# A Mamba-2 and FFN block on one core: Y turned by DVE and DMA in place of TensorE, the output projection in halves, part of the decay split on POOL

## The reference, cut to what matters

```python
xn = layernorm(x)                                  # x: (2, 2048, 512)
xb, z = split(xn @ in_proj_w.T)                    # 1024 each
xb = silu(causal_conv4(xb) + conv_b)
X, dt, B, C = split(xb @ x_proj_w.T)               # 16 heads of 64; B, C of 128
dt = softplus(dt @ dt_proj_w.T + dt_proj_b);  A = -exp(A_log) * dt
Y = scan of the state (decay exp(cumsum A), B, C, X * dt) + X * D
attn = (Y * silu(z)) @ out_proj_w.T                # 1024 -> 512
q(w) = clip(round(w / mean|w|), -1, 1)
ffn = (sigmoid(xn @ q(w1).T) * (xn @ q(w2).T)) @ q(w3).T    # 1408 hidden
out = x + attn + ffn
```

## Time and profile before

| | us |
|---|---|
| median of 3 runs | 1666.37 (1664.38 to 1667.06) |
| the profiled execution, its own time | 1663.81 |
| its span, first to last instruction | 1662.0 |
| busy in it: PE, DVE, ACT, POOL | 1600.7, 1126.5, 895.1, 540.0 |
| mean granted clock of TensorE | 0.987 of full |

### The profile page before, as it was taken

How to read it: one execution, slowest core, us unless ns; L and a number is a source line. 1 busy time by engine, 2 the same in 40 slices (tenths; PEclk the granted TensorE clock), 3 DMA queues, 4 the chain that set the end, 5 groups by cost and what they waited for, 6 DMA issues and landing times.

```text
span 1662.0 us, 25592 instructions
## 1 busy us (share of the span) xinstructions
PE 1600.7 (96%) x9430; PEld 785.2 (47%) x9430; DVE 1126.5 (68%) x1812; ACT 895.1 (54%) x1848; POOL 540.0 (32%) x502
## 2 busy tenths in 40 slices
PE   7778899999999999999999999999999999999999
PEld 3333444544444444445444454445444444444544
DVE  7876786687566764687656885568755676467762
ACT  6775526465356644476354663647535565357541
POOL 5236673243033421244121441314303242133320
PEclk9889899999999999999999999999999999999999
DMA  7144340111002110112001110011100111002100
GB/s 259 53 145 158 121 146 13 53 64 51 1 26 59 45 52 1 40 58 58 26 7 46 56 48 26 7 59 55 46 15 26 59 45 52 1 27 71 58 1 26
DMA packets 49277, 89.72 MB, mean 54 GB/s; under 512 B 6112, under 2 KB 7904, under 8 KB 49152
## 3 DMA queue, kind: packets, MB, share of 16 engines
q1 hardware_dynamic: 49152, 88.08, 16.5%
HBM read 79.41 MB, written 8.65 MB: 53 GB/s over the span
## 4 chain that ended last, share of the span: by engine, by line
PE 77%; issue 6%; ACT 6%; DVE 5%; POOL 2%; DMA 1%; SPq 0%; DVEq 0%; ACTq 0%; POOLq 0%
PE bank L612 18%; PE bank L522 13%; PE bank L630 9%; PE bank L416 9%; PE bank L432 8%; PE bank L589 7%; PE bank L442 4%; ACT edc L851 3%; PE bank L554 2%; PE bank L566 2%; PE bank L579 1%; PE bank L539 1%; POOL less L1508 1%; DVE edc L1204 1%; DVE mdc L1210 1%
## 5 line engine op out<-in xcount | busy, mean ns | idle before, releaser
L522 PE MATMUL bank<-wx_hi,arena 128*128 128x512 f16 x1024 | 319.3, 382 | 0.0
L612 PE MATMUL bank<-xt_lo,q 128*128 128x512 f16 x704 | 266.8, 379 | 0.0
L612 PE MATMUL bank<-xt_hi,q 128*128 128x512 f16 x704 | 266.8, 379 | 0.0
L1476 POOL TENSOR_TENSOR xst<-xdt,dst 128x512 f32<-128x512 f32 x64 | 66.8, 1043 | 530.1 <-DVE xdt L1158 530.1
L522 PE MATMUL bank<-wx_lo,arena 128*128 128x512 f16 x512 | 195.7, 382 | 0.0
L630 PE MATMUL bank<-q,arena 128*128 128x512 fp8e4 x704 | 163.2, 380 | 0.0
L851 ACT ACTIVATE edc<-csl,csv 128x128 f32<-128x128 f32 x512 | 155.8, 389 | 0.6 <-DMA csl<-sums 0.6
L522 PEld LDWEIGHTS bank<-wx_hi,arena 128*128 128x128 f16 x1024 | 101.0, 99 | 114.6 <-issue 3.4
L884 ACT CAST arena<-full 128x512 f16<-128x512 f32 x88 | 54.6, 620 | 148.1 <-DVE full L1261 148.1
L1204 DVE TENSOR_TENSOR edc<-edc,gt 128x512 f32<-128x512 f32 x128 | 88.2, 729 | 63.6 <-ACT edc L856 63.5
L1261 DVE SCALAR_TENSOR_TENSOR full<-tnh,bank 128x512 f32<-128x512 f32 x88 | 60.4, 687 | 96.3 <-PE bank L612 95.7
(11 more groups left out here) (202 smaller groups left out, 3563.3 us busy)
## 6 DMA issues: line engine op xcount, KB each, us to landing
csl<-sums SPq DMA_DIRECT2D x128, 256.0 KB, 3.3
raw<-w_ffn SPq DMA_DIRECT2D x34, 256.0 KB, 3.0
res<-x SPq DMA_DIRECT2D x32, 256.0 KB, 4.0
out<-res SPq DMA_DIRECT2D x32, 256.0 KB, 2.0
full<-w_ffn SPq DMA_DIRECT2D x24, 256.0 KB, 3.9
yac<-x SPq DMA_DIRECT2D x16, 256.0 KB, 2.7
gate<-x SPq DMA_DIRECT2D x16, 256.0 KB, 3.2
arena<-w_in SPq DMA_DIRECT2D x4, 512.0 KB, 7.4
```

The costliest lines, as they stand in the source:

```text
L522: i = pe.matmul(banks[0][:], act[:, k, c * P:(c + 1) * P], wt[:, k, hf * half:(hf + 1) * half], start=(n == 1), stop=(n == 3 * ki))
L612: i = pe.matmul(banks[2 * (m % 2) + j][:], q12[:, j, m, k, :], part[:, k, :], start=(n == 1), stop=(n == 2 * kd))
L1476: pool.tensor_tensor(by_head(xst[:], hd), by_head(xdt[:], hd), heads_over(sml["dst"][:, c, :], hf * hph, hph, hd), ALU.mult).then_inc(S["x ...
```

## The change

Block 0 keeps the old way, under the names `turn_first`, `project_first_out` and `split_y`. From block 1 on:

- DVE turns the 16 squares of 32x32 per 128 columns of `yac[u % 2]` in place into `ysq[u]` (the buffer `xs[u % 2]`), behind `project_x(u+1)`.
- SP, in unit `u + 1`, waits for that, stores the tile to DRAM (256 KB), waits until it has landed, and reads it back with 4 DMAs, one per 32 partitions, in runs of 32 float32 (128 B), into `yf[u]` (`yac[u % 2]`, for units 6 and 7 `xs[u % 2]`). That gives the full transpose.
- ACT (`split_y`, now behind `update` in unit `u + 1`) and DVE split it into hi and lo from SBUF; unit 7 follows at FFN step 4.
- PE makes no transposes of Y. `project_out(u)` is one half (12 matmuls) and comes two units later; the last two halves come behind FFN steps 2 and 6. DVE adds the sum to `res` at units 3, 5, 7 and FFN step 7.
- The lo part of the decay's group 1 is made by POOL (`decay`), not DVE. In all blocks the scale is put into `gt` once, so that both parts are plain copy and subtraction.

The diff, cut to its core:

```diff
+        ysq = [xs[u % 2] for u in range(len(units))]
+        yf = [yac[u % 2] if u < 6 else xs[u % 2] for u in range(len(units))]
+        y_dram = nc.dram_tensor("y_squares", [halves, P, half], F32, kind="Internal").ap()
...
+        def squares(dram, j):
+            return dram.rearrange("(i a) (k j b) -> j a k i b", a=SQ, b=SQ, j=P // SQ)[j]
+        def by_feature(t, j):
+            return t[j * SQ:(j + 1) * SQ, :].rearrange("a (k i b) -> a k i b", i=P // SQ, b=SQ)
...
+            def turn_y(b, u):                                   # SP
+                hf, n = u % 2, rounds(b, u)
+                sp.wait_ge(S["y_blocks"], at(b - 1, "y_blocks", u))
+                if n:
+                    sp.wait_ge(D[f"y_in{hf}"], n * (P // SQ) * DMA)
+                sp.dma_start(y_dram[hf], ysq[u][:]).then_inc(D[f"y_out{hf}"], DMA)
+                sp.wait_ge(D[f"y_out{hf}"], (n + 1) * DMA)
+                for j in range(P // SQ):
+                    sp.dma_start(by_feature(yf[u], j), squares(y_dram[hf], j)).then_inc(
+                        D[f"y_in{hf}"], DMA)
...
                 for u in range(len(units)):                     # SP
                     if u + 1 < len(units):
                         sums_in(b, u + 1)
+                    if b and u:
+                        turn_y(b, u - 1)
...
+                if b:
+                    turn_y(b, 7)
                 for m in range(kf):
...
+            def project_out(b, u):                              # PE
+                hf = u % 2
+                if u == 0:
+                    pe.wait_ge(S["acc"], at(b, "acc", 7))
+                elif hf == 0:
+                    pe.wait_ge(S["attn"], at(b, "attn", u // 2 - 1))
+                pe.wait_ge(S["yt_lo"], at(b, "yt_lo", u))
+                n = 0
+                for k in range(hf * per, (hf + 1) * per):
...
-                    if u and u % 2 == 0:
-                        project_out(b, u // 2 - 1)
+                    if b == 0 and u and u % 2 == 0:
+                        project_first_out(u // 2 - 1)
+                    elif b and u >= 2:
+                        project_out(b, u - 2)
...
+                    elif b and m in (2, 6):
+                        project_out(b, 6 if m == 2 else 7)
...
             def project_x(b, u):                                # ACT
                 act.wait_ge(S["x_mm"], at(b, "x_mm", u))
-                if u >= 2:
+                if u >= 2 and b:
+                    act.wait_ge(D[f"y_out{u % 2}"], rounds(b, u) * DMA)
+                elif u >= 2:
                     act.wait_ge(S["y_skip"], at(b, "y_skip", u - 2))
...
+            def split_y(b, u):                                  # ACT
...
+                    act.wait_ge(D[f"y_in{hf}"], (rounds(b, u) + 1) * (P // SQ) * DMA)
...
             def turn_y(b, u):                                   # DVE
+                dve.wait_ge(S["y_gated"], at(b, "y_gated", u))
+                dve.transpose(ysq[u][:], yac[u % 2][:]).then_inc(S["y_blocks"], 1)
+
+            def split_y(b, u):
                 hf = u % 2
                 ks = slice(hf * per, (hf + 1) * per)
                 dve.wait_ge(S["yt_hi"], at(b, "yt_hi", u))
+                src = yf[u][:] if b else banks[7][:]
...
                     if u + 1 < len(units):                      # DVE, unit loop
                         project_x(b, u + 1)
+                    if b:
+                        turn_y(b, u)
                     add_state(b, u)
                     if u + 1 < len(units):
                         update(b, u + 1)
                     aside()
-                    if u and u % 2 == 0:
+                    if b == 0 and u and u % 2 == 0:
                         project_out(b, u // 2 - 1)
+                    if u and b:
+                        split_y(b, u - 1)
                     if u + 2 < len(units):
                         project_z(b, u + 2)
                     split_state(b, u)
+                    if b and u >= 3 and u % 2:
+                        project_out(b, u // 2 - 1)
...
+            def decay(b, u):                                    # POOL
+                md = mdc[2 * (u % 2) + 1]
+                pool.wait_ge(S["m_hi"], at(b, "m_hi", 2 * u + 1))
+                pool.tensor_tensor(md[:, 1, :], edc[1][:], md[:, 0, :],
+                                   ALU.subtract).then_inc(S["m_lo1"], 1)
```

More of the change, by code:

```diff
@@ L16 @@
 DMA = 16
+SQ = 32
 XN_SCALE = 2.0 ** 5
@@ L121, in mamba_ffn_block @@
               *(f"early{n}" for n in range(4)),
-              *(f"beside{n}" for n in range(4)), "sums_out", "sums_in0", "sums_in1")}
+              *(f"beside{n}" for n in range(4)), "sums_out", "sums_in0", "sums_in1",
+             "y_out0", "y_out1", "y_in0", "y_in1")}
         def sb(name, shape, dt=F32):
@@ L581, in turn_y, with project_first_out @@
                 i.then_inc(S["y_turned"], 1)
-            def project_out(b, j):
-                pe.wait_ge(S["yt_lo"], at(b, "yt_lo", 2 * j + 1))
+            def project_first_out(j):
+                pe.wait_ge(S["yt_lo"], at(0, "yt_lo", 2 * j + 1))
                 n = 0
@@ L590, in project_out @@
                                       start=(n == 1), stop=(n == 3 * ki))
+                i.then_inc(S["first_out"], 1)
+            def project_out(b, u):
[7 more added lines that the diff above has]
+                for k in range(hf * per, (hf + 1) * per):
+                    for act, wt in passes(yt, wo):
+                        n += 1
+                        i = pe.matmul(banks[7][:], act[:, k, :], wt[:, k, :],
+                                      start=(hf == 0 and n == 1), stop=(hf == 1 and n == 3 * per))
                 i.then_inc(S["out_mm"], 1)
@@ L702, in tensor_program @@
                     ffn_up(b, m)
[L703 to L706, removed]
+                    if b == 0 and m == 0:
+                        turn_first(7)
+                    elif b == 0 and m == 1:
+                        project_first_out(3)
+                    elif b and m in (2, 6):
+                        project_out(b, 6 if m == 2 else 7)
                 if b < nb - 1:
@@ L862, in decay @@
                         act.wait_ge(S["s_lo"], at(b, "s_lo", 4 + 2 * u + g))
[L863 to L873, removed]
-                hf = u % 2
-                act.mul(yt[0][:, hf * per:(hf + 1) * per, :],
-                        banks[7][:].rearrange("p (k t) -> p k t", k=per), down).then_inc(S["yt_hi"], 1)
+                    act.copy(mdc[2 * (u % 2) + g][:, 0, :], edc[g][:]).then_inc(S["m_hi"], 1)
+            def split_y(b, u):
+                hf = u % 2
+                if b == 0:
+                    act.wait_ge(S["y_turned"], u + 1)
+                    if hf == 0 and u:
+                        act.wait_ge(S["first_out"], u // 2)
+                    src = banks[7][:]
+                else:
+                    act.wait_ge(D[f"y_in{hf}"], (rounds(b, u) + 1) * (P // SQ) * DMA)
+                    if u >= 2:
+                        act.wait_ge(S["out_mm"], at(b - 1, "out_mm", u - 2))
+                    elif b == 1:
+                        act.wait_ge(S["first_out"], chunks)
+                    else:
+                        act.wait_ge(S["out_mm"], at(b - 2, "out_mm", 6 + u))
+                    src = yf[u][:]
+                act.mul(yt[0][:, hf * per:(hf + 1) * per, :], src.rearrange("p (k t) -> p k t", k=per),
+                        down).then_inc(S["yt_hi"], 1)
             def hid_hi(b, m):
@@ L1218, in before_chunk @@
                     dve.wait_ge(S["dst"], at(b, "dst", 0))
-                if u >= 2:
-                    dve.wait_ge(S["y_turned"], at(b, "y_turned", u - 2))
+                if u >= 2 and b == 0:
+                    dve.wait_ge(S["y_turned"], u - 1)
+                elif u >= 2:
+                    dve.wait_ge(S["yt_lo"], at(b, "yt_lo", u - 2))
                 else:
```

85 lines of the change are left out of this document (49 added, 36 removed).

## The result

Slower: 1676.12 us median (1673.88 to 1676.42, 4 runs) against 1665.38 for the kernel before in the same comparison (1664.14 to 1667.06, 4 runs). The ratio is 1.0064, 95% interval 1.0052 to 1.0077. The forecast was 1645.5 and the range ended at 1668, so both missed. The profiled execution is 1676.19 us, its span 1674.1.

The account below looks back on a forecast made before the run. PE, busy 96% of the span, was taken as the bound. Units of 88.0 us against 90.66, plus 0.44 in the FFN, gave about 3.0 us per block, 21 in 7 blocks: 1645.5 us, range 1635 to 1668.

Parts of the forecast that it names:

- Steps 1 and 2: On PE: transposes leave, 3.5 us per block; output projection in halves, same work, 8 x 2.59 for 4 x 5.18.
- Step 4: DVE's transpose: 0.6 to 0.7 us, upper end 1.0; DVE's unit 10.75 us, under PE's 12.36.
- Step 3: Loop through ACT and DVE: 9.8 us, covered by PE's 13.0; wait before unit 2's scan stays 0.6.
- Step 5: POOL's part, one pass of 1.04 to 1.49 us: cost nothing; DVE's slack of 1.6 us takes lengthening up to 0.3.
- Step 6: Way through DRAM: costs PE nothing if in time; 9.9 us from transpose to landing, due after 10.3 in unit 6.
- rival A: Loads through DRAM: runs of 128 B are slow, 89 ns per packet, 17 us more per block, 1785; chance 0.17.
- B: DVE ends last, transpose at 1.0 or more and passes lengthened by POOL: 1 to 1.5 us per block, 1655; chance 0.15.

Follow-up runs that it names:

- gate_later: The changed kernel with DVE's gate pass of the next unit moved between yoff and the products from block 1 on; 1657.51 us, ratio 0.9959.
- short_decay2: The changed kernel with POOL's decay subtraction over 8 of 512 columns, PE multiplying the hi part again instead; 1653.55 us, ratio 0.9939.
- y_alone: The changed kernel without POOL's part, DVE making both low parts of the decay again; 1689.85 us, ratio 1.0155.
- turn_later: gate_later with DVE's transpose moved from ahead of the state's add to behind xst_lo; 1654.32 us, ratio 0.9938.
- no_squares: The changed kernel without DVE's transpose, yac itself being stored; 1659.8 us, ratio 0.9968.
- no_dram: The changed kernel without the DRAM store and four loads, so Y is turned inside the squares only; 1675.11 us, ratio 1.0064.
- short_skip: The changed kernel with POOL's add of the skip over 8 of 512 columns from block 1 on; 1652.13 us, ratio 0.9928.
- attn_later: turn_later with the adds to res of units 3 and 5 moved behind yoff of units 4 and 6; 1652.13 us, ratio 0.9926.

## Why the prediction was wrong

**Steps 1 and 2 held.** No float32 transpose is left behind block 0, the halves take 2.59 us each at full clock, and PE's busy time is 15 us down. That is under 7 x 3.5 because instructions under the lower clock count longer: in gate_later, where no block's clock falls, it is 1575.8, 24.9 down. PE's part of the gain was there to be had.

**Step 4 failed, in the sum for DVE's unit.** It said 10.99 - 0.60 - 0.54 + 0.65 + 0.25 = 10.75 and got 11.83. The transpose was well priced: 0.70 us, 0.63 from start to start. The Trainium skill (VectorE: DVE Perf Modes, The three transpose paths) gives 311 ns for 128x128 in bf16, and four of them would be an estimated 1.24; the measurement, on float32, is a little over half of that and decides. The term for shared SBUF was mis-sized: 0.25 was put on yt_lo, where nothing was lost (0.68). From start to start the products take 2.27 us in place of 1.47, the gated pass 1.13 in place of 0.61, xst_lo 1.25 in place of 0.85, state_lo 0.60 in place of 0.85: +1.47. I carried the widths of the passes over from the earlier trace rows and never laid POOL's timeline beside the new order of DVE's. Without yt_lo and the wait for exp between yoff and the products, the products had to fall into POOL's add, which starts at the end of yoff. Also, 10.75 was the unit without the add to `res`: 0.60 more in every second unit (12.4). The two kinds of unit average 12.13 us, so of the 1.6 us of slack against PE's 12.36 some 0.2 is left. PE therefore waits for nothing in units 3 to 6, and the loss shows behind the two units in which PE has only 9.77 us of work: before the scan of unit 2, and before scan and update of unit 7.

**Step 3 and the waits.** Unit 2's scan waits 1.53 us, not 0.6; unit 7's scan waits 1.02, not forecast at all; update(7) waits 1.64, not 1.0; the first scans of the block 0.7. Against the forecast's 88.0 us the eight units take 93.5 in block 3, 1.84 of it by the clock. The 3.7 that remain turn -3.0 per block into about +0.6.

**Step 5 failed.** "Cost nothing" came with the sentence that DVE's slack would take the longer passes. It takes them only if DVE has slack, and there was nearly none: short_decay2 is 23 us under the change. It still pays to have it on POOL (y_alone), since on DVE it would be 0.60 per unit more.

**Step 6 held, with room.** 7.0 us against 9.9. The new packets number 126,336 and took 24.6% x 16 x 1674.1 - 16.5% x 16 x 1662 = 2201 us, 17 ns each, stores of 2 KB included. The row of 45 ns that I took the earlier trace rows was far too dear, and rival A with it. The Trainium skill's read-modify-write below 512 B (DMA: Bandwidth & Descriptors, Specifications) gave A its chance; for these reads from DRAM into SBUF no such price is in the trace.

**The rivals.** B named the mechanism, DVE ends last with passes that POOL lengthens, and priced it at 1 to 1.5 us per block. It is 3.6 (from -3.0 to +0.58), and the clock adds 1.69 in four blocks of seven: 25 + 7 = 32 us, against 30.6 between forecast and median. The error that made the range miss is that DVE's rival stopped at 1655 and nothing slower than the kernel before was built on DVE, though the earlier trace rows have its loop at 10.99 us, 0.8 above PE's 10.2 in a unit without output projection.

## What to carry to other kernels

When a pass is moved or taken away on one of DVE and POOL, draw the other's timeline beside the new order, pass by pass: a pass with two SBUF inputs that starts beside one of POOL's takes 0.9 to 1.5 us in place of 0.68, by how much of POOL's pass is still to come, and two passes of another kind put in between give it back. A slack of 1.6 us in 12.4 is not a place to put work until both its longest unit and its stretched passes are counted. And where PE gets short waits close together, read the granted clock behind them: here that was more than half of the loss.

One place was left untried. In every unit DVE waits 0.70 us for ACT's xdt_hi ahead of xdt_lo, before and after, and the gated pass that the transpose needs is done by then. The transpose (0.63 from start to start) would fit there by these rows; no run has it there.

## What the runs showed of the hardware

- **DVE and POOL on SBUF.** A pair of float32 products is 1.29 us alone and 2.35 beside POOL's add, and that add is 1.28 without them and 1.65 with them; the gated pass 0.69 and up to 1.20. The transpose (0.70 in all kernels) and passes with one input in PSUM (0.65 to 0.69) show none of it. The Trainium skill (GPSIMD Engine Reference, 1. Specifications) says that GpSimd shares its SBUF interfaces with VectorE, with contention where a DVE instruction has two SBUF inputs; by that, the trace agrees: yt_lo too is 0.68 us where it meets no pass of POOL's, and 0.90 in turn_later, where it meets the state pass.
- **It reads as a wait, not as a slower pace.** In the unit shown the lengthened passes end a fixed time behind the pass of POOL's that they meet: the second product at 748.51 (POOL's add ends at 747.96), the gated pass at 750.94 (750.40), xst_lo at 755.66 (755.12), and yt_lo of no_squares at 749.39 (748.85). That is 0.54 or 0.55 us each time, whatever the start, as if the pass were held until POOL is done. POOL's add, in turn, starts 0.15 us behind the first product and takes 0.37 longer than alone.
- **Runs of 128 B** are cheap in reading: 64 KB in 512 runs land in 2.5 us, and four such loads, issued in 2.60 us, land 5.0 us after the first issue.
- **The clock falls behind short waits.** Between 800.83 and 804.34 us PE waited 1.02 us, made the 24 small matmuls of the scan, and waited 1.64; behind that it was granted the lower level (1.2 GHz) until 808. With the same waits at the same place of the block it fell in four blocks and stayed in three, in turn. What decides between them wasn't tried, and the turn is not fixed: in no_dram, with the same waits, it fell in blocks 2, 3, 5 and 7, and in y_alone, where the first wait is 2.37 us, in all seven. In gate_later, short_skip and short_decay2 the wait before update(7) is still 1.64, 1.52 and 1.51 us but the one before the scan is gone, and no block's clock falls; nor does it in turn_later, attn_later and no_squares.
